# Moving GpSimd's share of the states, the bf16 parts' transfers and the end-state copies of a selective scan

## The chip, the cores and the metric

The kernel runs on one core of one Trainium2 chip. The metric is the device time of one execution in microseconds (us). The core has five engines with a queue each: TensorE (PE), VectorE (DVE), ScalarE (ACT), GpSimd (POOL) and SyncE (SP, which only issues transfers). Each works its own queue in order and waits for the others by semaphores.

## The reference, cut to what matters

The whole network is an attention block, a sigmoid recurrence, a state-space block (Mamba) run forward and backward over 16384 tokens, and a two-of-eight expert block, each added to the input. The change touches only the state-space block, whose core is, for 128 inner channels and 16 states each:

```python
dt = softplus(dt @ dt_w.T + dt_b)
A = -exp(A_log)
dA = exp(dt[..., None] * A)
dBx = dt[..., None] * Bm[:, :, None, :] * xc[..., None]
def step(h, inp):
    dA_t, dBx_t, C_t = inp
    h = dA_t * h + dBx_t
    y = einsum('bds,bs->bd', h, C_t)
...
y = ys + xc * D
y = y * silu(z)
return y @ out_w.T
...
y_fwd + flip(mamba(flip(x)))
```

## The kernel before, in words

`scan_direction` is called twice, for the forward direction (tile names begin with `sf_`) and then the backward one (`sb_`). The 16384 tokens are cut into 16 chunks of 1024 (`TC`). Channels lie on the 128 partitions, tokens along the free axis. A chunk has 16 **units**, one for each state s. A unit consists of

- the decays exp(dt·A[s]), by ACT: `decay_v` (L1361) into the ring `dA`, three units ahead, or `decay_g` (L1366) into the PSUM buffer `pu`, one unit ahead;
- the inputs dt·x·B[s]. For the ten states in `BY_V`, PE spreads row s of B over the partitions with two bf16 matmuls into `pu` (`spread_b`, L1212), and DVE multiplies by `dtx` in place (`inject`, L1501). For the six states in `BY_G`, a transfer brings B's row spread into `bb`, and POOL multiplies into `dbx` (`inject`, L1436), two units ahead;
- the recurrence itself, by DVE: a scan instruction (L1521) that starts from `state[:, s]` and writes `h`, a ring of four;
- the product with C's row, by POOL: `read_c` (L1443) of unit s-1, into `hc`, a ring of four;
- the sum over the states, by PE: `total` (L1232), two matmuls with the identity into `py`, four units behind;
- the last column of `h`, kept for the next chunk, by ACT: `keep` (L1373).

`pu` has two PSUM buffers, used by s modulo 2. So `spread_b` and `decay_g` of unit s wait until the scan of unit s-2 is done; `spread_b` of unit 1 therefore waits for scan 15 of the chunk before.

Between the units stands the work that prepares the next chunk (`prepare`), with its place given by a unit number. The order on an engine is: the unit's own instructions, then `prepare`, then `tail`, then `own`. PE: the convolution (L1182, unit 0), B and C (`in_out`, units 2 and 3), the step size (units 5 and 6). ACT: `silu_x` after unit 1, in the backward direction `silu_z` too, between two table loads (L1285, L1292), since Silu and Exp are in different tables; `bc_rows` (4), `load_flat` (5), `part_high` (6), three pieces of softplus (7 and 8), `part_middle` (9), `store_parts` and `take_dt` (11), `load_parts` (12). POOL: `part_rest` (7), `linear_and_log` (9, L1417), `part_low` (10). DVE: `lost` (9), `step_sum` (10, L1476, which waits for POOL's `linear_and_log`), `dt_x` (12, L1482). B's rows are split into three bf16 parts, stored to memory and loaded back in another layout (`store_parts`, `load_parts`) for the matmuls of `spread_b`.

In the backward direction DVE also does `gate` (L1488) behind unit 3: it multiplies the finished y of the chunk before by silu(z). Only then may PE begin the next y. It does so in unit 4: the join with the forward y (L1224), the product with D (L1229) and `total` of unit 0; behind it stands the gate's matmul (`gate_in`, L1167). `project` (L1246) follows unit 13 on PE, `add_x` (L1494) unit 14 on DVE. In the forward direction ACT copies y out behind unit 3 (`take_y`).

The numbers that set the order:

```python
C_RING, B_RING, DECAY_RING = 4, 3, 5
DECAY_AHEAD, INJECT_AHEAD, LAG_SUM = 3, 2, 4
BY_G = (2, 5, 7, 10, 13, 15)
```

Of the kernel before, what the change touches and what calls it, by code (L numbers as in the profile page):

```python
# [24 lines left out]
def need(eng, sem, count):  # L25

    if not (isinstance(count, int) and count <= 0):
        eng.wait_ge(sem, count)  # L28
# [902 lines left out]
RING = 4  # L931
C_RING, B_RING, DECAY_RING = 4, 3, 5
DECAY_AHEAD, INJECT_AHEAD, LAG_SUM = 3, 2, 4
BY_G = (2, 5, 7, 10, 13, 15)
# [131 lines left out]
def scan_direction(nc, c, nd, k, way, y_scratch, rows, split):  # L1066
# [5 lines left out]
    U = STATES  # L1072
    NV, NG_ = len(BY_V), len(BY_G)
    with ExitStack() as ctx:
# [11 lines left out]
        h, hc = sb("h", [128, RING, TC]), sb("hc", [128, RING, TC])  # L1086
# [32 lines left out]
        def after(n, par, s):  # L1119

            return (n, par, s) if s < U else (n + 1, 1 - par, s - U)
# [153 lines left out]
        def _(act):  # L1275
# [88 lines left out]
            def decay_g(n, par, s):  # L1364
                need(act, scanned, n * U + s - 1)
                nc.scalar.activation(p_u[s % 2][:, :], dt[:, par, :], ACT.Exp,  # L1366
                                     scale=k["A"][:, s:s + 1]).then_inc(g_decayed, 1)

            def keep(n, s):

                act.wait_ge(scanned, n * U + s + 1)
                e = 0 if back else TC - 1
                nc.scalar.copy(state[:, s:s + 1], h[:, s % RING, e:e + 1]).then_inc(kept, 1)  # L1373
# [8 lines left out]
            def unit(n, par, s, first, last):  # L1382
                if first and s == 0:
                    for j in range(DECAY_AHEAD):
                        if j in BY_V:
                            decay_v(0, 0, j)
                m, mpar, ms = after(n, par, s + 1)
                if ms in BY_G and not (last and s == U - 1):
                    decay_g(m, mpar, ms)
                m, mpar, ms = after(n, par, s + DECAY_AHEAD)  # L1390
                if ms in BY_V and not (last and s + DECAY_AHEAD >= U):
                    decay_v(m, mpar, ms)
                if s >= 2:
                    keep(n, s - 2)
                elif not first:
                    keep(n - 1, s - 2 + U)
# [3 lines left out]
                       (8, softplus_exp), (8, softplus_one), (8, softplus_log), (9, part_middle), (11, store_parts),  # L1400
                       (11, take_dt), (12, load_parts)]
# [63 lines left out]
        def _(dve):  # L1465
# [38 lines left out]
            def unit(n, par, s, first, last):  # L1504
                if first and s == 0 and s in BY_V:
                    inject(0, 0, 0)
                u = n * U + s
                flow = lambda t: t[:, ::-1] if back else t[:, :]
                need(dve, kept, u + 1 - RING)
# [353 lines left out]
```

## Time and profile before

| what | us |
|---|---|
| median of 3 runs (2959.31 to 2975.59) | 2970.94 |
| the profiled execution | 2967.89 |
| its span in the profile | 2966.1 |
| PE busy | 2497.7 (84%) |
| DVE busy | 2318.3 (78%) |
| POOL busy | 2084.2 (70%) |
| ACT busy | 1576.8 (53%) |

The forward scans run from 851 to 1714 us of the span and the backward ones from 1763 to 2682 us, together about 60% of the time; everything outside them is unchanged. The busy shares over the whole span mix stages, so the two directions are to be read each for itself.

### The profile page before, as it was taken

To read this page: it belongs to the slowest core of one execution; us is meant where nothing else is said; L and a number is where in the kernel's file an instruction comes from. 1 tells how busy PE (TensorE), PEld (TensorE's weight loads), DVE (VectorE), ACT (ScalarE), POOL (GpSimd) and SP (SyncE) were. 2 spreads that over 40 slices of the span, in tenths; PEclk is the share of its full clock that TensorE was granted. 3 is DMA by queue.
4 is the path that set the end of the run, shared out by engine and by line. 5 is a ranking of instruction groups with operands and counts; after the bars stand their busy time and mean duration, and the time that the engine had idled before them with its cause. 6 is when DMAs were issued, how large, how long until landed. Compare 5 with 4: busy or idle time off the path is not lost. (4 is left out here: it accounts for less than half of the span.)

```text
span 2966.1 us, 34800 instructions
## 1 busy us (share of the span) xinstructions
PE 2497.7 (84%) x7800; PEld 1190.2 (40%) x7800; DVE 2318.3 (78%) x2487; ACT 1576.8 (53%) x2784; POOL 2084.2 (70%) x1166
## 2 busy tenths in 40 slices
PE   7899999957468988889889858899889889988598
PEld 7666666624322323323323223333333333336422
DVE  4366666560659999999999939998999899895499
ACT  6466666543655655555656446555555555545221
POOL 3133333230359999999999949999999999995155
PEclk6699999969779999999999889999999999997599
DMA  3000000000256777777777637776766676660022
GB/s 60 8 9 9 9 9 9 6 1 0 59 167 223 243 244 237 247 235 240 246 236 241 227 124 235 219 236 216 229 226 222 221 225 224 218 211 17 13 54 47
DMA packets 177295, 437.72 MB, mean 148 GB/s; under 512 B 65638, under 2 KB 70219, under 8 KB 177228
## 3 DMA queue, kind: packets, MB, share of 16 engines
q1 hardware_dynamic: 139340, 420.19, 44.5%
q10 hardware_dynamic: 37888, 16.79, 2.1%
q8 instruction: 24, 0.39, 0.1%
q14 instruction: 43, 0.35, 0.0%
HBM read 404.40 MB, written 24.12 MB: 144 GB/s over the span
## 5 line engine op out<-in xcount | busy, mean ns | idle before, releaser
L1443 POOL TENSOR_TENSOR sb_hc<-sb_h,sb_cc 128x1024 f32<-128x1024 f32 x256 | 599.7, 2360 | 61.8 <-PE sb_py L1232 56.2
L1443 POOL TENSOR_TENSOR sf_hc<-sf_h,sf_cc 128x1024 f32<-128x1024 f32 x256 | 595.8, 2347 | 11.5 <-DVE sf_h L1521 8.2
L1232 PE MATMUL sf_py<-sf_hc,ident 128*128 128x512 f32 x1024 | 533.1, 655 | 0.6 <-POOL sf_hc L1443 0.6
L1232 PE MATMUL sb_py<-sb_hc,ident 128*128 128x512 f32 x1024 | 519.5, 638 | 0.0
L572 POOL TENSOR_TENSOR ar_sc<-ar_sc,ar_mx 128x512 f32<-128x512 f32 x128 | 154.7, 1208 | 356.6 <-DVE ar_mx L513 356.6
L1521 DVE TENSOR_TENSOR_SCAN sf_h<-sf_dA,sf_state,sf_pu 128x1024 f32<-128x1024 f32 x160 | 375.4, 2346 | 19.1
L1521 DVE TENSOR_TENSOR_SCAN sb_h<-sb_dA,sb_state,sb_pu 128x1024 f32<-128x1024 f32 x160 | 375.2, 2345 | 17.1
L1232 PEld LDWEIGHTS sf_py<-sf_hc,ident 128*128 128x128 f32 x1024 | 197.0, 205 | 269.3 <-issue 239.8
L1232 PEld LDWEIGHTS sb_py<-sb_hc,ident 128*128 128x128 f32 x1024 | 187.3, 196 | 241.0 <-issue 232.0
L1501 DVE TENSOR_TENSOR sb_pu<-sb_pu,sb_dtx 128x1024 f32<-128x1024 f32 x160 | 193.9, 1212 | 52.7 <-PE sb_pu L1212 52.7
L1436 POOL TENSOR_TENSOR sb_dbx<-sb_dtx,sb_bb 128x1024 f32<-128x1024 f32 x96 | 226.5, 2359 | 3.3 <-DVE sb_dtx L1482 3.3
L1436 POOL TENSOR_TENSOR sf_dbx<-sf_dtx,sf_bb 128x1024 f32<-128x1024 f32 x96 | 225.2, 2346 | 3.3 <-DVE sf_dtx L1482 3.3
L1521 DVE TENSOR_TENSOR_SCAN sf_h<-sf_pu,sf_state,sf_dbx 128x1024 f32<-128x1024 f32 x96 | 223.7, 2330 | 1.8 <-ACT sf_state L1373 1.7
L1521 DVE TENSOR_TENSOR_SCAN sb_h<-sb_pu,sb_state,sb_dbx 128x1024 f32<-128x1024 f32 x96 | 223.9, 2332 | 0.0
L1212 PE MATMUL sf_pu<-sf_bcs,ss_sel 48*128 48x512 bf16 x320 | 104.9, 411 | 133.8 <-DVE sf_h L1521 117.0
L1361 ACT ACTIVATE sf_dA<-sf_dt,ss_A 128x1024 f32<-128x1024 f32 x160 | 182.3, 1141 | 55.6 <-DMA split_scratch<-sf_parts 47.4
L1361 ACT ACTIVATE sb_dA<-sb_dt,ss_A 128x1024 f32<-128x1024 f32 x160 | 182.4, 1141 | 53.7 <-DMA split_scratch<-sb_parts 40.3
L1501 DVE TENSOR_TENSOR sf_pu<-sf_pu,sf_dtx 128x1024 f32<-128x1024 f32 x160 | 194.0, 1212 | 10.4 <-PE sf_pu L1212 9.6
L1212 PE MATMUL sb_pu<-sb_bcs,ss_sel 48*128 48x512 bf16 x320 | 100.4, 396 | 116.1 <-DVE sb_h L1521 97.0
L1366 ACT ACTIVATE sf_pu<-sf_dt,ss_A 128x1024 f32<-128x1024 f32 x96 | 107.3, 1117 | 154.3 <-DVE sf_h L1521 119.0
L1366 ACT ACTIVATE sb_pu<-sb_dt,ss_A 128x1024 f32<-128x1024 f32 x96 | 107.2, 1117 | 148.8 <-DVE sb_h L1521 148.6
L508 DVE TENSOR_TENSOR ar_sc<-ar_pss,at_bias 128x512 f32<-128x512 f32 x128 | 88.5, 692 | 121.7 <-PE ar_pss L443 120.0
(294 smaller groups left out, 4594.6 us busy)
## 6 DMA issues: line engine op xcount, KB each, us to landing
sf_cc<-rows_scratch SPq DMA_DIRECT2D x256, 512.0 KB, 4.4
sb_cc<-rows_scratch SPq DMA_DIRECT2D x256, 512.0 KB, 4.4
sf_bb<-rows_scratch SPq DMA_DIRECT2D x96, 512.0 KB, 5.4
sb_bb<-rows_scratch SPq DMA_DIRECT2D x96, 512.0 KB, 5.4
sf_n<-n_scratch SPq DMA_DIRECT2D x32, 258.0 KB, 5.4
sb_n<-n_scratch SPq DMA_DIRECT2D x32, 258.0 KB, 5.3
y_scratch<-sf_yo SPq DMA_DIRECT2D x16, 512.0 KB, 6.1
sb_yf<-y_scratch SPq DMA_DIRECT2D x16, 512.0 KB, 5.1
```

The costliest lines, as they stand in the source:

```text
L508: nc.vector.tensor_tensor(sc[:, j, :, :], ps_s[:, j % 2, :, :], bias[:, :, :], ALU.add).then_inc(added, 1)
L572: nc.gpsimd.tensor_tensor(sc[:, j, :, :], sc[:, j, :, :], mx[:, j, :].rearrange("p (h a) -> p h a", a=1).to_broadcast([128, HEADS, 128]), ...
L1212: ins = nc.tensor.matmul(p_u[s % 2][:, hf], lhsT=k["sel"][:, s:s + 1].to_broadcast([3 * STATES, 128]), rhs=bcs[:, par, hf], start=True, st ...
L1232: ins = nc.tensor.matmul(p_y[:, hf], lhsT=c.ident[:, :], rhs=hc[:, s % RING, hf], start=False, stop=(s == U - 1))
L1361: nc.scalar.activation(dA[:, BY_V.index(s) % DECAY_RING, :], dt[:, par, :], ACT.Exp, scale=k["A"][:, s:s + 1]).then_inc(v_decayed, 1)
L1366: nc.scalar.activation(p_u[s % 2][:, :], dt[:, par, :], ACT.Exp, scale=k["A"][:, s:s + 1]).then_inc(g_decayed, 1)
L1436: nc.gpsimd.tensor_tensor(dbx[:, r % B_RING, :], dtx[:, par, :], bb[:, r % B_RING, :], ALU.mult).then_inc(g_injected, 1)
L1443: nc.gpsimd.tensor_tensor(hc[:, s % RING, :], h[:, s % RING, :], cc[:, s % C_RING, :], ALU.mult).then_inc(read, 1)
L1501: nc.vector.tensor_tensor(p_u[s % 2][:, :], p_u[s % 2][:, :], dtx[:, par, :], ALU.mult).then_inc(v_injected, 1)
L1521: nc.vector.tensor_tensor_scan(out=flow(h[:, s % RING, :]), data0=flow(decays), data1=flow(inputs), initial=state[:, s:s + 1], op0=ALU.mul ...
```

## The change

GpSimd's six states become 0, 3, 6, 9, 11 and 14. ACT keeps end states two at a time, in every odd unit, ahead of `decay_v` instead of behind it. `take_dt` goes ahead of `store_parts`, which goes from unit 11 to unit 12, and `load_parts` from 12 to 14.

```diff
-BY_G = (2, 5, 7, 10, 13, 15)
+BY_G = (0, 3, 6, 9, 11, 14)
...
             def decay_g(n, par, s):
+                if s == 0:
+                    act.wait_ge(dt_done, n + 1)
                 need(act, scanned, n * U + s - 1)
...
-                act.wait_ge(scanned, n * U + s + 1)
+                act.wait_ge(scanned, n * U + s + 2)
                 e = 0 if back else TC - 1
-                nc.scalar.copy(state[:, s:s + 1], h[:, s % RING, e:e + 1]).then_inc(kept, 1)
+                nc.scalar.copy(state[:, s:s + 2], h[:, s % RING:s % RING + 2, e]).then_inc(kept, 1)
...
                 if ms in BY_G and not (last and s == U - 1):
                     decay_g(m, mpar, ms)
+                if s % 2 and s >= 3:
+                    keep(n, s - 3)
+                elif s % 2 and not first:
+                    keep(n - 1, s - 3 + U)
                 m, mpar, ms = after(n, par, s + DECAY_AHEAD)
                 if ms in BY_V and not (last and s + DECAY_AHEAD >= U):
                     decay_v(m, mpar, ms)
-                if s >= 2:
-                    keep(n, s - 2)
-                elif not first:
-                    keep(n - 1, s - 2 + U)
...
-                       (8, softplus_exp), (8, softplus_one), (8, softplus_log), (9, part_middle), (11, store_parts),
-                       (11, take_dt), (12, load_parts)]
+                       (8, softplus_exp), (8, softplus_one), (8, softplus_log), (9, part_middle),
+                       (11, take_dt), (12, store_parts), (14, load_parts)]
...
-                need(dve, kept, u + 1 - RING)
+                if s % 2 == 0:
+                    need(dve, kept, n * PAIRS + (s - RING) // 2 + 1)
```

Lines of the changed kernel are one to six higher than those of before.

ScalarE, backward direction, around the two table loads of a chunk. Before:

```order
L1366 ACTIVATE sb_pu<-sb_dt,ss_A 128x1024
L1361 ACTIVATE sb_dA<-sb_dt,ss_A 128x1024
L1373 COPY sb_state<-sb_h 128x1
L1285 ACT_TABLE_LOAD
L1285 ACTIVATE sb_xc<-sb_pp,ss_cb 128x1024
L1289 ACTIVATE sb_zs<-sb_zs 128x1024
L1292 ACT_TABLE_LOAD
L1373 COPY sb_state<-sb_h 128x1
L1361 ACTIVATE sb_dA<-sb_dt,ss_A 128x1024
```

The same place in the changed kernel:

```order
L1362 ACTIVATE sb_dA<-sb_dt,ss_A 128x1024
L1376 COPY sb_state<-sb_h 128x2
L1362 ACTIVATE sb_dA<-sb_dt,ss_A 128x1024
L1286 ACT_TABLE_LOAD
L1286 ACTIVATE sb_xc<-sb_pp,ss_cb 128x1024
L1290 ACTIVATE sb_zs<-sb_zs 128x1024
L1293 ACT_TABLE_LOAD
L1369 ACTIVATE sb_pu<-sb_dt,ss_A 128x1024
L1362 ACTIVATE sb_dA<-sb_dt,ss_A 128x1024
```

The decays into `pu` next to this place were those of unit 2, ahead of the table loads; now they are those of unit 3, right behind them.

TensorE, backward direction, where the next y begins (L1224, L1225). Before:

```order
L1201 MATMUL sb_pp<-sb_xc,ss_wbc 32x512
L1224 MATMUL sb_py<-sb_yf,ident 128x512 x2
L1229 MATMUL sb_py<-sb_xc,ss_dg 128x512 x2
L1232 MATMUL sb_py<-sb_hc,ident 128x512 x2
L1167 MATMUL sb_pp<-sb_n,ss_wz 128x512 x2
L1212 MATMUL sb_pu<-sb_bcs,ss_sel 128x512 x2
L1232 MATMUL sb_py<-sb_hc,ident 128x512 x2
```

The same place in the changed kernel:

```order
L1202 MATMUL sb_pp<-sb_xc,ss_wbc 32x512
L1213 MATMUL sb_pu<-sb_bcs,ss_sel 128x512 x2
L1225 MATMUL sb_py<-sb_yf,ident 128x512 x2
L1230 MATMUL sb_py<-sb_xc,ss_dg 128x512 x2
L1233 MATMUL sb_py<-sb_hc,ident 128x512 x2
L1168 MATMUL sb_pp<-sb_n,ss_wz 128x512 x2
L1233 MATMUL sb_py<-sb_hc,ident 128x512 x2
```

The spread of B's row for the next DVE state (`pu`) stood behind the new y (unit 6); now one stands ahead of it (unit 5) and the next one follows further down (unit 7).

GpSimd, backward direction, the second half of a chunk. Before:

```order
L1436 TENSOR_TENSOR sb_dbx<-sb_dtx,sb_bb 128x1024
L1443 TENSOR_TENSOR sb_hc<-sb_h,sb_cc 128x1024 x3
L1423 TENSOR_TENSOR sb_rest<-sb_flat,sb_parts 128x128
L1436 TENSOR_TENSOR sb_dbx<-sb_dtx,sb_bb 128x1024
L1443 TENSOR_TENSOR sb_hc<-sb_h,sb_cc 128x1024 x2
L1417 TENSOR_TENSOR sb_tc<-sb_tc,sb_tb 128x1024
```

The same place in the changed kernel:

```order
L1448 TENSOR_TENSOR sb_hc<-sb_h,sb_cc 128x1024 x3
L1441 TENSOR_TENSOR sb_dbx<-sb_dtx,sb_bb 128x1024
L1448 TENSOR_TENSOR sb_hc<-sb_h,sb_cc 128x1024
L1428 TENSOR_TENSOR sb_rest<-sb_flat,sb_parts 128x128
L1448 TENSOR_TENSOR sb_hc<-sb_h,sb_cc 128x1024
L1441 TENSOR_TENSOR sb_dbx<-sb_dtx,sb_bb 128x1024
L1448 TENSOR_TENSOR sb_hc<-sb_h,sb_cc 128x1024
L1422 TENSOR_TENSOR sb_tc<-sb_tc,sb_tb 128x1024
```

Before, `dbx` of unit 7 stood ahead of the three reads of units 4, 5 and 6, and `dbx` of unit 10 between the reads and `linear_and_log` (`sb_tc`). Now the reads of units 3, 4 and 5 come first, and both `dbx` of unit 9 and `dbx` of unit 11 stand between the read of unit 5 and `linear_and_log`.

## Rows read from the trace of the kernel before

**Rows 1.** Windows, forward and backward scans: busy us of each engine, PEclk, DMA

```profile
900.00:1700.00 800.00, 690.89 (x1524) 243.99 (x1524) 761.76 (x428) 450.74 (x670) 795.19 (x368) 0.93 0.73 239
1800.00:2640.00 840.00, 741.42 (x1833) 285.96 (x1832) 774.12 (x450) 465.14 (x666) 788.34 (x364) 0.95 0.69 224
```

**Rows 2.** Waits, 1860 to 2580: who waited, us in total, times, longest

```profile
ACT sb_dt L1322 <- POOL sb_parts L1428: 57.0, 12, 4.8
POOL sb_hc L1443 <- PE sb_py L1232: 44.4, 44, 1.9
DVE sb_pu L1501 <- PE sb_pu L1212: 40.7, 12, 3.4
```

**Rows 3.** Timeline of DVE, one backward chunk: start us, us, instruction, idle before

```profile
2234.04 1.22 DVE L1488 TENSOR_TENSOR sb_yo<-sb_py,sb_zs 128x1024 f32<-128x1024 f32 x1 [0.57 <-PE sb_py L1232]
2235.18 2.34 DVE L1521 TENSOR_TENSOR_SCAN sb_h<-sb_dA,sb_state,sb_pu 128x1024 f32<-128x1024 f32 x1
2237.44 2.32 DVE L1521 TENSOR_TENSOR_SCAN sb_h<-sb_pu,sb_state,sb_dbx 128x1024 f32<-128x1024 f32 x1
2243.19 1.23 DVE L1501 TENSOR_TENSOR sb_pu<-sb_pu,sb_dtx 128x1024 f32<-128x1024 f32 x1 [3.43 <-PE sb_pu L1212]
...
2260.80 1.22 DVE L1476 TENSOR_TENSOR sb_pp<-sb_tc,sb_pp 128x1024 f32<-128x1024 f32 x1
...
2265.52 2.35 DVE L1521 TENSOR_TENSOR_SCAN sb_h<-sb_dA,sb_state,sb_pu 128x1024 f32<-128x1024 f32 x1
...
2275.34 2.34 DVE L1521 TENSOR_TENSOR_SCAN sb_h<-sb_pu,sb_state,sb_dbx 128x1024 f32<-128x1024 f32 x1
...
2291.77 1.21 DVE L1488 TENSOR_TENSOR sb_yo<-sb_py,sb_zs 128x1024 f32<-128x1024 f32 x1
```

**Rows 4.** Timeline of PE, the same backward chunk

```profile
2222.71 3.60 PE L1182 MATMUL sb_pp<-sb_n,ss_taps 128*128 128x512 f32 x8
...
2235.40 1.98 PE L1224 MATMUL sb_py<-sb_yf,ident 128*128 128x512 f32 x4 [0.52 <-DVE sb_yo L1488]
...
2240.74 1.98 PE L1167 MATMUL sb_pp<-sb_n,ss_wz 64*128 64x512 f32 x4
2242.56 0.59 PE L1212 MATMUL sb_pu<-sb_bcs,ss_sel 48*128 48x512 bf16 x2
2243.09 1.98 PE L1232 MATMUL sb_py<-sb_hc,ident 128*128 128x512 f32 x4
```

**Rows 5.** Timeline of ACT, the same backward chunk

```profile
2226.47 1.28 ACT L1285 ACT_TABLE_LOAD   x1 [1.26 <-PE sb_pp L1182]
2227.76 1.11 ACT L1285 ACTIVATE sb_xc<-sb_pp,ss_cb 128x1024 f32<-128x1024 f32 x1
...
2229.84 1.28 ACT L1292 ACT_TABLE_LOAD   x1
...
2232.39 1.12 ACT L1366 ACTIVATE sb_pu<-sb_dt,ss_A 128x1024 f32<-128x1024 f32 x1
```

**Rows 6.** Timeline of POOL, the same backward chunk

```profile
2245.22 2.36 POOL L1443 TENSOR_TENSOR sb_hc<-sb_h,sb_cc 128x1024 f32<-128x1024 f32 x1 [1.92 <-PE sb_py L1232]
...
2250.49 2.38 POOL L1436 TENSOR_TENSOR sb_dbx<-sb_dtx,sb_bb 128x1024 f32<-128x1024 f32 x1
...
2257.45 2.37 POOL L1417 TENSOR_TENSOR sb_tc<-sb_tc,sb_tb 128x1024 f32<-128x1024 f32 x1
```

**Rows 7.** Timeline of POOL, one forward chunk

```profile
1211.27 2.34 POOL L1417 TENSOR_TENSOR sf_tc<-sf_tc,sf_tb 128x1024 f32<-128x1024 f32 x1
...
1250.94 6.97 POOL L1443 TENSOR_TENSOR sf_hc<-sf_h,sf_cc 128x1024 f32<-128x1024 f32 x3
```

**Rows 8.** Timeline of DVE, the same forward chunk

```profile
1213.65 1.23 DVE L1476 TENSOR_TENSOR sf_pp<-sf_tc,sf_pp 128x1024 f32<-128x1024 f32 x1 [0.44 <-POOL sf_tc L1417]
```

**Rows 9.** Timeline of PE, the same forward chunk

```profile
1230.21 0.60 PE L1212 MATMUL sf_pu<-sf_bcs,ss_sel 48*128 48x512 bf16 x2
...
1246.48 1.88 PE L1232 MATMUL sf_py<-sf_hc,ident 128*128 128x512 f32 x4
```

More of the change, by code:

```diff
@@ L1073, in scan_direction @@
     NV, NG_ = len(BY_V), len(BY_G)
+    PAIRS = U // 2
     with ExitStack() as ctx:
@@ L1383, in unit @@
                 if first and s == 0:
+                    if s in BY_G:
+                        decay_g(0, 0, s)
                     for j in range(DECAY_AHEAD):
```

## The prediction, made before the changed kernel was run

> **What bounds the kernel now.** I read the page first: no engine is busy over the whole span, and the chain that ended last runs through the experts' stage and says nothing here. So I took windows of the two scan directions [rows 1]. Forward, POOL is busy for 795 of 800 us: it sets the pace, and nothing that frees another engine can make this direction faster, since POOL's work is the same before and after (22 products and the three pieces for the next chunk). Backward, POOL (788 of 840) and DVE (774) both have gaps. The waits say why [rows 2]: POOL waits for PE's y sums, 44.4 us in 12.5 chunks, and DVE once in each chunk, for 3.4 us, for PE's spread of B. The timelines show this place. DVE does `gate` at 2234.04 [rows 3]; only then PE begins the next y, at 2235.40, then comes `gate_in` at 2240.74, and then the spread of unit 6, at 2242.56 [rows 4]. Meanwhile DVE has only scans 4 and 5 and stands until 2243.19. From one gate to the next are 2291.77 - 2234.04 = 57.73 us, my backward period. It is made of 26.76 (gate to `step_sum` at 2260.80), 4.72 (to scan 12), 9.82 (to scan 15) and 16.43 (to the gate).
>
> **Prices.** A scan holds DVE for 2.26 (2235.18 to 2237.44). From scan 15 to the gate are five scans and four injects, so these take 16.43 - 5 x 2.26 = 5.13: 1.34 for an inject whose own scan follows at once, 1.12 with something else between. A POOL product takes 2.32 (2250.49 to 2257.45 are three) [rows 6]; its short pieces, about 0.4, are in both orders. On PE a spread takes 0.53 and a sum of four records 1.82 [rows 4]. A `decay_g` takes 1.12 on ACT [rows 5].
>
> **The change, part by part.**
>
> *Behind the gate, DVE.* It now has scan 4, inject 5, scan 5 and scan 6 ahead of the first inject (7) that needs a spread behind the new y: 2.26 + 1.34 + 2.26 + 2.26 = 8.1 us in place of 4.5. But that spread also stands further back, behind the sum of unit 1 and a step-size half (about 0.9). So PE frees inject 7 not 9.1 us after the gate's start but about 11.9, and the wait is 11.9 - 1.1 - 8.1 = 2.7 instead of 3.4. This is all that the regular spacing wins there, 0.7 us, and only if DVE is what sets the period.
>
> *Behind the gate, POOL.* The read of unit 5 needs the sum of unit 1. That sum now follows `gate_in` directly: gate + 1.36 + 5.34 + 1.82, and the read starts 2.13 behind the sum's start [rows 4, 6], at gate + 10.65 (before: 11.18). Then POOL has read 5, product 9, read 6, the rest piece, read 7, product 11, read 8: six products and 0.4, or 14.3 us, one product more than before, because the product of 7 used to be done while POOL waited. `linear_and_log` starts at gate + 24.95, and `step_sum` 2.38 behind its start (as forward, 1211.27 to 1213.65 [rows 7, 8]): gate + 27.33 instead of 26.76. **+0.6.** DVE alone, freed at gate + 11.9, would be there 1.4 us earlier, so its 0.7 is lost again.
>
> *From `step_sum` to scan 12*: one scan, one inject and the sum itself in both, 4.72. *From scan 12 to scan 15*: DVE gets injects 13 and 15 where it had 14: 2.26 + 1.12 + 1.12 + 2.26 + 2.26 + 1.12 + 0.6 (`add_x`) = 10.74 instead of 9.82. **+0.9.** It is paid back with one inject fewer behind scan 15, if nothing stops DVE there.
>
> *From scan 15 to the gate.* Something does. PE may spread unit 1 only when scan 15 is done, 2.41 us after its start; spread and a sum (0.53 + 1.82) put the convolution at +4.76. ACT's first table load came 3.76 behind the convolution's start (2222.71 to 2226.47), the second 3.37 later, and what follows it 1.29 later [rows 4, 5]. Before, no decay that DVE needs soon stood behind: that of unit 2 was ahead of the loads. Now `decay_g` of unit 3 is the first instruction behind them: 4.76 + 3.76 + 3.37 + 1.29 + 1.12 = 14.3 us after scan 15's start, when scan 3 may begin. DVE's own work would be there after four scans and two injects, 4 x 2.26 + 2.68 = 11.7. So DVE waits 2.6 for ACT, in a place where it never waited. (PE's spread of unit 2, now behind the convolution, is late by 0.7 too; the longer wait holds it.) Then scan 3 and inject 4: the gate is at 14.3 + 2.26 + 1.12 = 17.7 instead of 16.43. **+1.3.**
>
> Sum backward: 27.33 + 4.72 + 10.74 + 17.7 = 60.5, against 57.73: **+2.8 a chunk**.
>
> *The table loads, by a page.* Rows 5 show the load itself at 1.28 and the next ACTIVATE 1.29 behind its start. The Trainium skill, "ScalarE: Activation LUTs", section "What ACT_TABLE_LOAD costs", gives about 2.66 us for every switch, drain included. With two switches ahead of `decay_g` of unit 3 the wait would be 2.8 longer (an estimate from that page), a period of 63.3. The row speaks against it; it is rival D.
>
> *Forward.* Counted from the start of `linear_and_log` (1211.27), read 4 of the next chunk started at 1250.94, +39.67 [rows 7], with POOL never idle. In the new order one product fewer stands before it, so POOL is there at +37.36. It needs the sum of unit 0. Before, from the spread of unit 1 (1230.21) to that sum's end (1246.48 + 1.88) PE needed 18.15 without a gap [rows 9]; now there is one spread more in it (unit 5), 18.7. The spread starts at 2.38 (`step_sum` [rows 8]) + 15.1 (`step_sum` itself, scans 11 to 14, injects 12, 13 and 15 and `dt_x`: 1.12 + 4 x 2.26 + 1.34 + 1.12 + 1.12 + 1.34) + 2.41 = +19.9, before +18.94. The sum ends at 38.6 and POOL reads at 38.7: POOL waits 1.4 us where it had 2.6 us in hand. Nothing gives it back. DVE's wait for `decay_g` of unit 3 is 1.5 here (no silu of z between the tables), and its cycle of about 53.9 stays under 55.3. **+1.4 a chunk** on 53.9.
>
> *The rest.* `take_dt` no longer waits for POOL's last part; it waited 57.0 us in 12.5 chunks [rows 2], but dt is ready by scan 12 in both orders, so this is worth nothing on the path. The two transfers of the parts are still issued from ACT's queue, a unit or two later, and what stands behind `load_parts` there is `decay_g` of unit 0, needed three scans later; PE first needs the parts for unit 1 of the next chunk, after scan 15. I take nothing for it; if the store had not landed by unit 14, its remainder would go straight onto scan 0. Half as many `keep`s free a little of ACT, which it doesn't need. The two-at-a-time wait asks, ahead of scan s, for the copy of scan s-3, and ACT gets to it within one unit: nothing again. Without that cover a late copy could hold each even scan by up to a decay's 1.12.
>
> **The sum.** Sixteen chunks have 15 intervals in a direction; the first starts with empty rings, so I count 14. Backward 14 x 2.8 = 39, forward 14 x 1.4 = 20: 2968 + 59 = 3027 for the profiled execution, which is 3 under the median. With a microsecond or so off each direction's start (scan 0 no longer needs the bf16 parts) I say **3025**.
>
> **The rivals.**
> A, the forecast, 0.50: 3005 to 3045 as the terms come out 40% smaller or larger.
> B, only the backward direction slows, 0.16: forward POOL's 1.4 us is a difference of sums of 38 us, and PE's clock and gaps can move it by that much. 2968 + 39 = 3007.
> C, scan 3 doesn't wait for ACT (convolution or silu is earlier than I place it), 0.12: then only PE's 0.7 at unit 2 is left there, the gate is at 15.9, the period 58.7, +1.0 a chunk or 14, with 0 to 20 forward: 2982 to 3002, say 2992.
> E, even, 0.10: POOL's waits behind the gate end as they did; 2968.
> F, faster, 0.10: one mechanism, DVE's longer cover behind the gate. If neither `step_sum` nor scan 3 waits, DVE sets the period and wins 0.7 a chunk, 14 x 0.7 = 10, 2958; if PE frees inject 7 before DVE is there, 3.4 x 14 = 48, 2920. It decides from the point where PE needs less than 9.2 us from the gate's start to the spread of unit 7; the rows give 11.9.
> D, the page's table switch, 0.02: backward 5.6 and forward about 2.8 a chunk, 3085.
>
> **How the numbers follow.** A, B and C and part of E lie within **2970 to 3045**, which leaves out F, D and the edges. A measurement of this kernel can tell about 0.5% (15 us) from no change. Faster by more: most of F, 0.08. Within: E, the rest of F and the low end of C, 0.14. Slower by more: 0.78.
>
> **What would show it.** Right: in the backward chunk a wait of DVE at scan 3 for ACT's decay, some 2 to 3 us, that isn't there before; a wait of about 1 us at `step_sum` for POOL; the wait for the spread still 2 to 3 us, now at inject 7; POOL's waits for the sums at reads 4 and 5 up from 3.4 to over 6 us; a period of about 60.5. Forward, POOL busy 97 to 98% instead of 99.4%, with one wait of 1 to 1.5 us for PE, period about 55.3. Wrong: scans back to back through units 0 to 3, or POOL still full forward. The weakest step is the place of the convolution against scan 15: all of +1.3 hangs on it, and the forward term on the same spread of unit 1.

## The result and the profile after

The changed kernel takes 3052.66 us (median of four runs, 3040.46 to 3054.44) against 2965.12 of the kernel before on the same chip (2951.19 to 2975.59): ratio 1.029, 95% interval 1.024 to 1.034. It is slower, as forecast, but by 3% instead of 2%; the time is 8 us above the top of the range. The profiled execution has a span of 3052.7 us, 86.6 more than before. In a second set the ratio was 1.029 again (1.025 to 1.034).

The windows of the two directions, with the columns of [rows 1]. POOL is busy for 769 of 800 us forward, where it was busy for 795, and for 653 of 740 us backward, where it was busy for 788 of 840:

```profile
900.00:1700.00 800.00, 684.24 (x1477) 243.19 (x1478) 736.55 (x414) 429.22 (x540) 769.28 (x357) 0.92 0.70 230
1900.00:2640.00 740.00, 642.80 (x1543) 242.96 (x1544) 643.89 (x376) 375.82 (x459) 653.26 (x303) 0.93 0.65 212
```

The waits, 1900 to 2640, answer to [rows 2]: who waited, us in total, times, longest.

```profile
POOL sb_hc L1448 <- PE sb_py L1233: 86.7, 36, 4.5
...
ACT sb_dt L1323 <- DVE sb_pp L1481: 50.4, 12, 4.2
...
DVE sb_pu L1506 <- PE sb_pu L1213: 49.6, 24, 2.7
...
DVE sb_h L1527 <- ACT sb_pu L1369: 21.1, 12, 1.8
...
DVE sb_pp L1481 <- POOL sb_tc L1422: 15.7, 12, 1.3
```

The last two are new: once in each chunk at scan 3 for ACT's decay (1.8), and once at `step_sum` for POOL (1.3). `take_dt` now waits for DVE, no longer for POOL's parts. One backward chunk and the first scans of the next, on DVE; it answers to [rows 3]:

```profile
2217.57 2.34 DVE L1527 TENSOR_TENSOR_SCAN sb_h<-sb_dA,sb_state,sb_pu 128x1024 f32<-128x1024 f32 x1
...
2226.57 1.23 DVE L1506 TENSOR_TENSOR sb_pu<-sb_pu,sb_dtx 128x1024 f32<-128x1024 f32 x1 [0.81 <-PE sb_pu L1213]
...
2232.04 2.35 DVE L1527 TENSOR_TENSOR_SCAN sb_h<-sb_pu,sb_state,sb_dbx 128x1024 f32<-128x1024 f32 x1 [1.75 <-ACT sb_pu L1369]
...
2235.43 1.21 DVE L1493 TENSOR_TENSOR sb_yo<-sb_py,sb_zs 128x1024 f32<-128x1024 f32 x1
...
2247.37 1.23 DVE L1506 TENSOR_TENSOR sb_pu<-sb_pu,sb_dtx 128x1024 f32<-128x1024 f32 x1 [2.63 <-PE sb_pu L1213]
...
2262.73 1.23 DVE L1481 TENSOR_TENSOR sb_pp<-sb_tc,sb_pp 128x1024 f32<-128x1024 f32 x1 [1.30 <-POOL sb_tc L1422]
...
2267.47 2.35 DVE L1527 TENSOR_TENSOR_SCAN sb_h<-sb_dA,sb_state,sb_pu 128x1024 f32<-128x1024 f32 x1
...
2278.18 2.35 DVE L1527 TENSOR_TENSOR_SCAN sb_h<-sb_dA,sb_state,sb_pu 128x1024 f32<-128x1024 f32 x1
...
2288.76 1.23 DVE L1506 TENSOR_TENSOR sb_pu<-sb_pu,sb_dtx 128x1024 f32<-128x1024 f32 x1 [2.39 <-PE sb_pu L1213]
...
2294.23 2.35 DVE L1527 TENSOR_TENSOR_SCAN sb_h<-sb_pu,sb_state,sb_dbx 128x1024 f32<-128x1024 f32 x1 [1.76 <-ACT sb_pu L1369]
...
2297.61 1.22 DVE L1493 TENSOR_TENSOR sb_yo<-sb_py,sb_zs 128x1024 f32<-128x1024 f32 x1
```

From scan 15 at 2217.57 to the gate at 2235.43 are 17.86 us, from the next scan 15 (2278.18) to its gate (2297.61) 19.43. The two passages of scan 15 on PE show where the 1.57 us are:

```profile
2220.06 0.59 PE L1213 MATMUL sb_pu<-sb_bcs,ss_sel 48*128 48x512 bf16 x2 [0.94 <-DVE sb_h L1527]
2220.58 1.98 PE L1233 MATMUL sb_py<-sb_hc,ident 128*128 128x512 f32 x4
2222.40 3.60 PE L1183 MATMUL sb_pp<-sb_n,ss_taps 128*128 128x512 f32 x8
...
2280.58 0.89 PE L1213 MATMUL sb_pu<-sb_bcs,ss_sel 48*128 48x512 bf16 x2 [1.98 <-DVE sb_h L1527]
2281.40 3.35 PE L1233 MATMUL sb_py<-sb_hc,ident 128*128 128x512 f32 x4
2284.59 3.60 PE L1183 MATMUL sb_pp<-sb_n,ss_taps 128*128 128x512 f32 x8
```

The same spread and the same sum take 2.3 us once and 4.0 the next time; the convolution starts 4.83 and 6.41 behind scan 15. The granted clock of the two stretches (the last number but two):

```profile
2218.00:2222.00 4.00, 3.06 (x9) 1.02 (x8) 4.00 (x2) 1.52 (x3) 4.00 (x3) 1.00 0.56 134
2280.50:2284.60 4.10, 4.02 (x7) 1.53 (x8) 3.97 (x4) 1.24 (x2) 4.10 (x3) 0.58 0.95 351
```

The first is all at 2.4 GHz, the second mostly at 1.2, which I call half clock from here on; a chunk or period without it on the path I call clean. ACT, and with it scan 3, is late by the same amount. In front of scan 3 ACT shows what was forecast, compare [rows 5]:

```profile
2226.16 1.28 ACT L1286 ACT_TABLE_LOAD   x1 [4.96 <-PE sb_pp L1183]
...
2229.53 1.28 ACT L1293 ACT_TABLE_LOAD   x1
2230.82 1.12 ACT L1369 ACTIVATE sb_pu<-sb_dt,ss_A 128x1024 f32<-128x1024 f32 x1
```

I took every interval from one `step_sum` to the next in the two traces. Backward, before, they are 57.6 to 57.7 or, in every second chunk from the sixth on, 58.4 to 58.5, but for the first (57.3); after, they are 60.6 or 62.27, from the third on in turn, but for the first (58.9) and the last (60.9). In all seven of 60.6 the convolution starts 4.8 us behind scan 15, in all five of 62.27 it starts 6.4 behind. In the first and the last ACT's first table load runs ahead of the convolution's end, 3.6 us behind scan 15, and scan 3 waits for ACT only 0.38 us instead of 1.76. Forward, after, five of 14 are 55.3, with the convolution at 4.8; nine are 56.1 or 57.0, with it at 5.4 to 6.5. The whole span, in us:

| stretch | before | after | more | forecast |
|---|---|---|---|---|
| start to the first `step_sum` | 844.5 | 851.3 | 6.7 | 0 |
| first forward interval | 41.9 | 44.0 | 2.2 | 0 |
| 14 forward intervals | 758.7 | 786.5 | 27.8 | 20 |
| to the first backward `step_sum` | 111.2 | 107.1 | -4.1 | 0 |
| first backward interval | 41.9 | 48.0 | 6.1 | 0 |
| 14 backward intervals | 810.7 | 855.5 | 44.7 | 39 |
| the rest | 357.2 | 360.3 | 3.2 | 0 |

### The profile page after: what moved, and what is told of

The parts are those of the page before. It is cut to its first block and busy times, and to the rows that moved or that the text cites. A ratio compares the mean times of both kernels' runs of the same rounds, so it can differ in the third digit from the quotient of the medians.

```text
span 3052.7 us, 34204 instructions
## 1 busy us (share of the span) xinstructions
PE 2549.1 (84%) x7800; PEld 1211.6 (40%) x7800; DVE 2317.0 (76%) x2487; ACT 1549.3 (51%) x2530; POOL 2082.5 (68%) x1166
## 5 line engine op out<-in xcount | busy, mean ns | idle before, releaser
L1448 POOL TENSOR_TENSOR sb_hc<-sb_h,sb_cc 128x1024 f32<-128x1024 f32 x256 | 600.0, 2356 | 111.2 <-PE sb_py L1233 107.7
L1233 PE MATMUL sb_py<-sb_hc,ident 128*128 128x512 f32 x1024 | 533.9, 661 | 0.0
L1233 PEld LDWEIGHTS sb_py<-sb_hc,ident 128*128 128x128 f32 x1024 | 197.8, 206 | 270.6 <-issue 262.0
L1369 ACT ACTIVATE sf_pu<-sf_dt,ss_A 128x1024 f32<-128x1024 f32 x96 | 107.1, 1116 | 158.6 <-DVE sf_h L1527 156.4
```

The costliest lines, as they stand in the source:

```text
L1233: ins = nc.tensor.matmul(p_y[:, hf], lhsT=c.ident[:, :], rhs=hc[:, s % RING, hf], start=False, stop=(s == U - 1))
L1448: nc.gpsimd.tensor_tensor(hc[:, s % RING, :], h[:, s % RING, :], cc[:, s % C_RING, :], ALU.mult).then_inc(read, 1)
```

## The experiments

Ratios are to the kernel before in the same set (medians there 2960.6 to 2964.1). "F" and "B" are the sums of the 14 forward and 14 backward intervals of a kernel's trace: 758.7 and 810.7 before, 786.5 and 855.5 after. Ahead of these intervals most experiments change nothing, and yet the first `step_sum` lay between 837 and 855 us: differences under some 10 us of the whole are read from F and B, not from the time.

**The places alone.** The kernel before with the six new places and nothing else but what they need.

```diff
-BY_G = (2, 5, 7, 10, 13, 15)
+BY_G = (0, 3, 6, 9, 11, 14)
@@ decay_g
+                if s == 0:
+                    act.wait_ge(dt_done, n + 1)
```

> The kernel before with only GpSimd's units moved to 0, 3, 6, 9, 11, 14 (and the wait of unit 0's decay that this needs). My theory: the places alone make the whole loss, by what they put behind the table loads, behind the gate and ahead of linear_and_log: about 3050 us, forward period 55.3 to 57, backward 60.6 to 62.3. Rival: the moved store, load and take_dt or the end states kept in pairs carry a part of it: below 3030.

Measured: ratio 1.023 (1.021 to 1.025), F 786.4, B 849.4. By this trace the places carry all of F's loss and 39 of B's 45; by the medians, 72 of the 88 us. The profiled execution is the longest of the four (3054.0; the others 3030.0 to 3039.7), so the split is rough. Its backward chunks are also of two kinds that the changed kernel doesn't mix like this. In six, ACT's first table load stands behind the convolution, scan 3 waits 1.76, and the clean period is 60.6, as in the changed kernel. In eight, the load runs while ACT waits for the convolution, scan 3 waits 0.35, and the clean period is 59.2:

```profile
2348.85 1.28 ACT L1285 ACT_TABLE_LOAD   x1
2354.74 1.11 ACT L1285 ACTIVATE sb_xc<-sb_pp,ss_cb 128x1024 f32<-128x1024 f32 x1 [4.60 <-PE sb_pp L1182]
...
2413.99 1.28 ACT L1285 ACT_TABLE_LOAD   x1 [5.94 <-PE sb_pp L1182]
2415.28 1.11 ACT L1285 ACTIVATE sb_xc<-sb_pp,ss_cb 128x1024 f32<-128x1024 f32 x1
```

Half clock in five chunks (60.9 to 64.0) makes up for it. An estimate from the clean periods alone, 8 x 59.2 + 6 x 60.6 = 837, gives the places 30 and ACT's queue 11 of the 42 us by which clean backward chunks grew. Why the load stands now ahead of ACT's wait and now behind it isn't shown.

**ACT's queue alone.** The changed kernel with the old places.

```diff
-BY_G = (0, 3, 6, 9, 11, 14)
+BY_G = (2, 5, 7, 10, 13, 15)
```

> The changed kernel with GpSimd's units back at 2, 5, 7, 10, 13, 15, so only ScalarE's queue is changed (store_parts, load_parts, take_dt, end states in pairs, kept ahead of decay_v). My theory: nothing, within 8 us of the kernel before, periods 53.9 and 57.6 to 58.5. Rival: a part of the loss is here, 10 us or more above it; or a gain, now that ACT does not stand 4.8 us ahead of dt.

Measured: ratio 1.001 (0.9995 to 1.003), F 753.8, B 810.6, periods 53.9 and 57.6 / 58.4. The later transfers, the kept pairs and the earlier `take_dt` are worth nothing here as a whole; F is 5 us shorter than before, all of it in one interval (53.0 for 57.85, the one with half clock described further down). With the new places the queue adds 6 us to B (849.4 to 855.5): scan 3 waits 1.76 for ACT in 12 of 14 chunks, instead of 0.96 on average (1.76 in six, 0.35 in eight).

**The table loads one unit later**, behind the decay of unit 3.

```diff
-            prepare = [(1, silu_x), ...
+            prepare = [(2, silu_x), ...
-                run(act, unit, prepare, [(1, silu_z)], [(1, exp_log_tables), (5, take_z)])
+                run(act, unit, prepare, [(2, silu_z)], [(2, exp_log_tables), (5, take_z)])
```

> The changed kernel with silu_x, silu_z and the second table load placed after unit 2 instead of unit 1, so that the decay of unit 3 stands ahead of them. My theory: DVE's wait for that decay (1.76 us backward, 0.7 to 0.8 forward) is gone, the backward gate comes 1.3 us sooner until PE's late spreads and sums stop it, forward nothing since POOL's read of unit 4 binds: 3030 to 3040 us. Rival: the wait is cover for PE's late spread and its removal only lengthens the wait at the gate or at inject 7: 3050.

Measured: ratio 1.024 (1.022 to 1.026), F 786.4, B 840.9. DVE waits for ACT no more; clean backward periods fall from 60.6 to 59.4, by 1.2 of the 1.3 that the forecast had put there. There are five of these. Eight others are 60.6 again: there the convolution is at 5.4 to 6.5, and DVE waits 2.5 us at inject 2 instead of 0.74.

**`linear_and_log` one unit earlier.**

```diff
-            run(pool, unit, [(7, part_rest), (9, linear_and_log), (10, part_low)])
+            run(pool, unit, [(7, part_rest), (8, linear_and_log), (10, part_low)])
```

> The changed kernel with POOL's linear_and_log after unit 8 instead of unit 9, so ahead of dbx of unit 11 and the read of unit 8. My theory: step_sum no longer waits for POOL (1.3 us backward, 1.0 forward); backward DVE wins 1.3 a chunk; forward DVE gets ahead by 1 us, so spread 1, sum 0 and POOL's read 4 come sooner and the period falls from 55.3 to about 54.2: together 3015 us. Rival: POOL's time to log is not there earlier or the time is lost again at the gate: 3045 to 3052.

Measured: ratio 1.020 (1.017 to 1.024), F 786.0, B 836.4, clean backward periods 59.2. The wait at `step_sum` is gone, and clean periods are 1.4 shorter: the 0.6 of the forecast against the kernel before, and the 0.7 and more that DVE alone could have won ("1.4 us earlier"). Forward the third to the eighth period are 54.2 to 54.8, but from the ninth on they are 57.3 to 58.2: POOL now waits for ACT's softplus, 28.0 us in 10 chunks.

**The changed kernel again**, as the reference of the next three.

> The changed kernel again, unaltered, as the reference for the three others of this call. Both theories: about 3040 to 3055 us, ratio to before 1.024 to 1.030, periods 55.3 to 57.0 forward and 60.6 / 62.3 in turn backward. How far its clean periods and its whole time differ from the first run shows how much of the whole time is not in the chunks.

Measured: 3050.02 us, ratio 1.029 (1.025 to 1.034), F 786.6, B 855.4, the same alternation.

**Zero matmuls against the clock, first try.** They add zeros to the running y.

```diff
+            def fill(s):
+                if s in (1, 12, 13, 15):
+                    for _ in range(6):
+                        nc.tensor.matmul(p_y[:, 0:HALF], lhsT=nil[:, 0:128], rhs=nil[:, :], start=False, stop=False)
@@ spread_b
+                fill(s)
                 need(pe, scanned, n * U + s - 1)
```

> The changed kernel with six matmuls of a zero tile, added into the running y (they add zeros), ahead of the spreads of units 1, 12, 13 and 15 in every chunk, where PE stands idle. Clock theory (the 1.6 us that every second chunk takes beyond the forecast is PE at half its clock behind these gaps, on the path from scan 15 over the spread of unit 1 and the convolution to ACT and scan 3): periods uniform, 55.3 forward and 60.6 backward, no stretch of these chunks with PEclk near 0.5, the 14 intervals 786 -> 775 forward and 855 -> 848 backward, time 18 us or so lower, 3030 to 3038. Rival (the alternation is a beat of waits between the engines, and the clock only follows): periods alternate as before whatever the clock says, time unchanged or some us longer, as the zero matmuls delay the spread by what they overhang.

Measured: ratio 1.036 (1.032 to 1.041), F 801.0, B 863.3. A miss. Six take 1.47 us. Ahead of unit 1 that is a little more than PE's idle time: backward the convolution is at 5.1 in most chunks, and behind scan 15 the clock is full there, as wanted. But in four chunks DVE waits 4.3 to 4.4 us at inject 7 instead of 2.7, since now the join of y behind the gate runs partly at half clock (3.51 us at 2120.86 instead of 1.98). Forward, from the seventh period on, the convolution is at 7.4 to 7.5 and the periods are 57.9 to 58.1.

The same in the kernel before, ahead of units 0, 1, 12 and 14:

> The kernel before with the same zero matmuls, ahead of the spreads of units 0, 1, 12 and 14. Clock theory: the backward periods, 57.64 and 58.45 in turn, become 57.64 throughout, so 5 to 6 us less, and forward stays at 53.9, where POOL is never idle: ratio 0.998. Rival: no change in the alternation. With this and the run above the cost of the change at a full clock can be read: 2.9 a chunk backward and 1.4 forward by the forecast's terms, 60 us, against 72 measured in the chunks.

Measured: ratio 1.023 (1.019 to 1.028), F 766.5, B 854.4. Also a miss: ahead of units 0 and 1 PE wasn't idle at all here, and backward the convolution is at 6.4 to 8.3 behind scan 15 instead of 5.0. It shows something else, though. With 2.6 us more on PE ahead of the convolution (two fills of 1.3) B is 44 longer, 3 a chunk (60.2 in two chunks, 61.4 to 61.5 in eleven in which half clock came on top): PE's stretch behind scan 15 was nearly on the path before, too.

**Table loads and `linear_and_log` together.** The edits of the third and fourth experiment.

> The changed kernel with both waits that the forecast named put off: the table loads and silus one unit later (behind the decay of unit 3) and POOL's linear_and_log one unit earlier (unit 8). Alone, the first gave 841 backward and 786 forward over 14 intervals, the second 836 and 786. If the two terms are independent and add (the forecast's sum: +1.3 at scan 3, +0.6 at step_sum): backward 855 - 15 - 19 = 821, forward 786, time about 3013 to 3020. Rival (each was only the last of several waits, and PE's y sums and spreads behind the gate come next): backward stays near 836 and the time near 3024.

Measured: ratio 1.023 (1.019 to 1.027), F 809.3, B 815.2, most backward periods 57.9 to 58.1. Backward both waits are gone, and 40 of the 45 us come back, more than the 15 and 19 of each alone. Forward POOL waits for ACT, 50.4 us in 13 chunks.

**The convolution first.** In PE's queue it goes ahead of the spread of unit 1, into the time in which PE waits for scan 15.

```diff
             def unit(n, par, s, first, last):
+                if s == 0 and not last:
+                    for step in (convolve(halves[0]), convolve(halves[1])):
+                        step(n + 1, 1 - par)
                 m, mpar, ms = after(n, par, s + 1)
@@ in the loop over units (ahead of it the steps stay)
-            prepare = [(0, convolve(a)), (0, convolve(b)), (2, in_out(a)), (3, in_out(b)),
+            prepare = [(-1, convolve(a)), (-1, convolve(b)), (2, in_out(a)), (3, in_out(b)),
```

> The changed kernel with one move on PE: the next chunk's convolution stands ahead of the spread of unit 1, which waits for scan 15, instead of behind that spread and the sum after it. So it fills PE's gap of 0.9 to 2.0 us there, and neither the sum of 1.98 us (3.35 at half clock) nor the wait for scan 15 lies between it and ACT's table loads any more; what it overhangs makes the spread of unit 1 about 1.5 to 2 us later. Theory (backward: scan 3 waits for ACT behind the convolution, and the 1.6 us of every second chunk is the half clock of the sum on this path; forward: POOL waits for the sum of unit 0 at the end of PE's chain from scan 15): no wait of DVE for ACT at scan 3, backward periods 58.8 to 59.4 without the alternation, 14 intervals 823 to 832 instead of 855; forward POOL full again, periods 53.9 to 54.5, 14 intervals 755 to 763 instead of 786; time about 3000. Rival 1 (the alternation is a beat between POOL and PE behind the gate): the backward periods still alternate by about 1.6. Rival 2 (forward, the six-product order itself costs POOL 1.4): forward stays near 786 and the time near 3025.

Measured: ratio 1.010 (1.007 to 1.013), F 775.3, B 813.9: backward more than expected, forward less. Backward the period is 57.8 to 58.1 in all chunks but the first, without the alternation by 1.6, and DVE has no wait for ACT. Half clock is still there. In the last seven chunks it takes in all of PE's work from the spread of unit 12 to the `...` here (granted clock 0.57 from 2226.0 to 2237.5), though no longer the two sums just ahead of the convolution:

```profile
2226.07 1.03 PE L1213 MATMUL sb_pu<-sb_bcs,ss_sel 48*128 48x512 bf16 x2 [2.51 <-DVE sb_h L1530]
2227.03 3.78 PE L1233 MATMUL sb_py<-sb_hc,ident 128*128 128x512 f32 x4
2230.86 1.03 PE L1213 MATMUL sb_pu<-sb_bcs,ss_sel 48*128 48x512 bf16 x2
2231.83 5.70 PE L1233 MATMUL sb_py<-sb_hc,ident 128*128 128x512 f32 x8
...
2239.72 3.70 PE L1233 MATMUL sb_py<-sb_hc,ident 128*128 128x512 f32 x8
2243.26 3.60 PE L1183 MATMUL sb_pp<-sb_n,ss_taps 128*128 128x512 f32 x8
2246.79 0.60 PE L1213 MATMUL sb_pu<-sb_bcs,ss_sel 48*128 48x512 bf16 x2
```

These chunks are 58.0 to 58.1, the six before them, with less of it, 57.8 to 57.9. So half clock costs next to nothing by itself: it costs where PE is on the path. Forward five periods are 54.0 to 54.3, as POOL alone would have it, the others up to 57.3: the theory's gain came in a third of the chunks.

**The same in the kernel before.**

> The kernel before with the same move of the convolution. Forward POOL is never idle, so nothing: 53.9. Backward, by the clock theory, the alternation of 57.64 and 58.45 ends at 57.64 or a little less: 14 intervals 807 or under instead of 810.7, ratio 0.998 to 1.000. Rival (the later spread of unit 1 is needed at once by inject 1 or holds POOL's next sum): backward 1 to 2 us a chunk longer, ratio 1.005 to 1.01.

Measured: ratio 1.013 (1.009 to 1.016), F 760.3, B 833.1. The rival: backward inject 1 waits 0.8 to 2.2 us for the later spread; most periods are 58.6, and three times 61.7 with 60.0 behind it, where half clock comes on top. The old places want the spread of unit 1 at once.

**Convolution first, `linear_and_log` earlier in the backward direction alone.**

```diff
-            run(pool, unit, [(7, part_rest), (9, linear_and_log), (10, part_low)])
+            run(pool, unit, [(7, part_rest), (8 if back else 9, linear_and_log), (10, part_low)])
```

> The first kernel of this call with POOL's linear_and_log one unit earlier (8 for 9) in the backward direction alone. With silu and linear_and_log moved together the backward periods were 57.9 to 58.1 throughout, 815 in 14 intervals, though the forward ones rose to 58 from a new wait. Theory: both waits that the forecast named are gone here without that side effect: backward 812 to 818, forward 755 to 763, time 2985 to 2992, still not under before, since PE frees the inject behind the gate as late as before (57.6 or so a chunk). Rival (with DVE's five units behind the gate the period falls under that of before once the two waits are gone, the case F of the forecast): backward under 807, time under 2980.

Measured: ratio 1.009 (1.006 to 1.012), F 773.1, B 812.6, periods of 56.48 and 59.58 in strict turn. The chunk of 59.58 on PE, just ahead of its convolution:

```profile
2293.53 0.60 PE L1213 MATMUL sb_pu<-sb_bcs,ss_sel 48*128 48x512 bf16 x2 [2.51 <-DVE sb_h L1530]
2294.06 3.34 PE L1233 MATMUL sb_py<-sb_hc,ident 128*128 128x512 f32 x4
...
2305.00 1.03 PE L1213 MATMUL sb_pu<-sb_bcs,ss_sel 48*128 48x512 bf16 x2
2305.96 6.49 PE L1233 MATMUL sb_py<-sb_hc,ident 128*128 128x512 f32 x8
2312.28 3.60 PE L1183 MATMUL sb_pp<-sb_n,ss_taps 128*128 128x512 f32 x8
```

In the chunk of 56.48 the two sums ahead of the convolution take 3.70, here 6.49; DVE then stands 3.06 us at inject 1 for the spread behind it, where it doesn't wait in the short chunk.

**The mixed kernel.** Forward the old places and the old order, backward as in the last kernel.

```diff
+    BY_G = (0, 3, 6, 9, 11, 14) if back else (2, 5, 7, 10, 13, 15)
+    BY_V = tuple(s for s in range(16) if s not in BY_G)
```

> Forward as in the kernel before (its places of GpSimd's units, the convolution behind the first sum), backward as in the last kernel of the call before (new places, convolution first, linear_and_log at unit 8), where chunks of 56.5 and 59.6 took turns. Theory: forward 753 to 759 in 14 intervals, backward 812 or so, first backward interval 48 instead of 42; time 2968 to 2980, the same as before within what can be told. Rival (the forward half clocks and the queue changes cost here too): over 2985.

Measured: 2968.38 us, ratio 1.002 (1.000 to 1.003), F 753.8, B 803.5. Six periods are 56.4 to 56.5 in a row, then come six of 58.0 to 58.1 and one of 56.7. The backward instructions stand in the same order as in the kernel just above, with B = 812.6: 9 us apart by where half clock fell. Against the kernel before, B is 7 us shorter, the first backward interval 5.6 longer (47.5), and the whole the same, as expected.

**Zero matmuls only in idle time**, first in the mixed kernel (backward):

```diff
+                for _ in range({12: 11, 13: 3}.get(s, 0) if back else 0):
```

> The same with zero matmuls in the backward direction where TensorE stands idle: eleven ahead of the spread of unit 12 (idle 2.51) and three ahead of that of unit 13 (0.85). Clock theory: chunks of 56.5 throughout, 14 intervals 791 to 796 instead of 812, time 2948 to 2960, which is the case F of the forecast with its two waits and the clock taken away. Rival (59.6 isn't from the clock, or filled gaps don't hold the clock up): 812 or more, time as the mixed kernel without fills or above it.

Measured: ratio 1.003 (1.002 to 1.005), B 812.5, periods 56.5 and 59.6 in strict turn: no gain. The fill ended half clock behind units 12 and 13, but in every second chunk the two sums just ahead of the convolution still take 6.5 us instead of 3.7.

Then in the kernel before, ahead of units 11, 12 and 14 (`{11: 5, 12: 3, 14: 15}`):

> The kernel before with zero matmuls only where TensorE is idle: five ahead of the spread of unit 11 (idle 1.33), three ahead of unit 12 (0.85), fifteen ahead of unit 14 (3.87). Clock theory: backward periods 57.64 throughout (14 intervals 807 instead of 810.7), forward 53.9, granted clock of these windows up from 0.94 and 0.95, time 4 us lower. Rival: the half clock comes all the same, periods 57.64 and 58.45 in turn.

Measured: ratio 1.002 (1.000 to 1.004), F 757.0, B 811.2. Eleven of the 13 last backward periods are 57.6 to 57.7, but one is 58.95 and one 60.68. Half clock still came once with only 0.53 us idle, right behind fifteen zero matmuls:

```profile
2257.25 3.41 PE L1209 MATMUL sb_py<-sb_nil 48*128 48x512 bf16 x15
2261.18 1.03 PE L1219 MATMUL sb_pu<-sb_bcs,ss_sel 48*128 48x512 bf16 x2 [0.53 <-DVE sb_h L1530]
```

And in the changed kernel, `{12: 11, 13: 5, 1: 4}`:

> The changed kernel with zero matmuls only where TensorE is idle: eleven ahead of the spread of unit 12 (2.51), five ahead of unit 13 (1.3 to 2.3), four ahead of unit 1 (0.9 to 2.0). Clock theory: periods 55.3 and 60.6 throughout, 14 intervals 775 and 848 instead of 787 and 855, time 3030 to 3036. Rival: the alternation stays and the time is 3050 or above.

Measured: ratio 1.032 (1.026 to 1.037), F 788.1, B 858.8. The convolution now starts 4.75 behind scan 15 in 13 of 14 backward chunks, and most periods still are 60.6 and 62.2 in turn; forward the fill delays it to 5.6 to 7.2 in eight chunks. PE at another place of the long chunk, the join of y behind the gate, and DVE behind it:

```profile
2246.30 3.68 PE L1232 MATMUL sb_py<-sb_yf,ident 128*128 128x512 f32 x4 [1.59 <-DVE sb_yo L1502]
...
2258.67 1.23 DVE L1515 TENSOR_TENSOR sb_pu<-sb_pu,sb_dtx 128x1024 f32<-128x1024 f32 x1 [4.32 <-PE sb_pu L1220]
```

The join takes 3.68 in place of 1.98, and the wait at inject 7 is 4.32 in place of 2.70. The half clock has moved from one place of the path to another.

## Why the prediction was right in direction and too low

**Which case.** A, waits in both directions, is what happened; its range of 3005 to 3045 ended too low.

**Gate to `step_sum`** was 27.33, measured 27.30 (2235.43 to 2262.73). Its cause, six products of POOL behind the late sum, stands in the wait of 1.30 and in the fourth experiment. (POOL's waits for the sums at reads 4 and 5 are 4.42 and 1.48 us, 5.9 together; over 6 was expected.) DVE alone would be there 1.4 us earlier, as forecast. **`step_sum` to scan 12**: 4.72, measured 4.74. **Scan 12 to scan 15**: 10.74, measured 10.71. **Scan 15 to the gate**: 17.7, measured 17.86 in a clean chunk. The wait of 2.6 came as 0.81 at inject 2 and 1.75 at scan 3; the forecast gave all of it to scan 3. Scan 3 starts at 14.47 (forecast 14.3). The sum, 60.5, is 60.62 in clean chunks. **Behind the gate** the wait for the spread is 2.63 at inject 7 (forecast 2.7). **Forward** 55.3, measured 55.27 in clean chunks; the forecast's own difference, 38.7 - 37.36, is 1.34 and not 1.4, and 1.34 is what clean chunks show.

Clean against clean, 14 x (60.62 - 57.65) + 14 x (55.27 - 53.93) = 60.3 us, where the forecast had 59. Rivals B, C and E fall with it. F's mechanism does exist, though not in this change: with both waits gone and the convolution first, clean chunks last 56.4 to 56.5, under the 57.65 before; in no kernel were all chunks like that.

**The step that failed** is the convolution's place against scan 15, "spread and a sum (0.53 + 1.82) put the convolution at +4.76", taken as the same in every chunk. The forecast named this step its weakest, but gave TensorE's clock no term; rival B mentions it, as something that could take away 1.4 us, not add. In every second backward chunk the spread and sum run at half clock, on the path, and the convolution is at +6.4. Before, half clock also came, backward in every second chunk from the sixth on, but there it cost 0.8 us:

```profile
2209.40:2214.00 4.60, 4.55 (x7) 1.66 (x8) 4.49 (x3) 2.43 (x4) 4.60 (x3) 0.50 0.69 242
```

Forward, before, it cost something in one chunk alone: in the interval of 57.85 PE ran at a granted clock of 0.50 from 900.5 to 909.7, and DVE waited 3.91 us for a spread. In the others POOL set the pace. The new places put this stretch of PE on the path in both directions, with the whole delay. What lies above the clean periods is 6.8 backward (before 3.6) and 12.7 forward (before 3.7, all of it in that one interval): 12 us net.

The Trainium skill, "TensorE: Matmul & The Clock Gate", Part 1 on the clock gate, says that the number of slow matmuls varies from run to run with the phase of the gate. The traces agree: in two executions of the changed kernel the longer forward intervals fall on different chunks (the fourth is the first of them in one, the third in the other), and two kernels with one backward order, the mixed one and the one before it, had B of 803.5 and 812.6.

**The remainder.** Of 86.6 us the forecast had 59. Missing are 12 for the clock, 1.3 in the clean periods, 8 in the first intervals and 6 outside the chunks. The 6 can't be told from chance: the forward scans' first instruction, ahead of which nothing was changed, already runs at 814.7 before and 822.3 after, and between 808 and 825 in the 17 traces.

The 8 are a second step that failed: "with a microsecond or so off each direction's start" measured 2.2 and 6.1 more. The first backward interval is 46.6 to 49.0 in every kernel with the new places backward, and 41.9 to 42.8 with the old ones in the old order. Most of it is one wait, 4.5 to 5.3 us in all kernels with the new places, where the kernel before has none at inject 6 or 7 of this interval:

```profile
1821.46 1.23 DVE L1506 TENSOR_TENSOR sb_pu<-sb_pu,sb_dtx 128x1024 f32<-128x1024 f32 x1 [4.53 <-PE sb_pu L1213]
```

There is no gate in this interval. PE begins the join of y 19.6 us behind the `step_sum` instead of 16.5, since now the spread of unit 5, which waits for scan 3, stands ahead of it, and the join takes 3.78 us instead of 1.98. The other waits are 0.75 at inject 2 for PE and 1.35 at the next `step_sum` for POOL. The kernel before with the convolution first (46.9) has waits for PE at other places, 3.23 at inject 1 and 1.59 at inject 6.

**The range.** By its own rule, terms 40% larger, it would have ended at 2968 + 1.4 x 59 = 3051. Its top of 3045 allows for 30%. The measured time is 2 us above the former and 8 above the latter.

**Right on the rest with the old places alone**: there the later transfers, the kept pairs and `take_dt` cost nothing. With the new ones, for which the forecast took nothing for them either, they cost 6 us of B by the traces and 11 by the estimate from clean periods, all at scan 3. The clean period came out right because the chain had the first table load behind the convolution, as it stood in the kernel before; with the places alone it stands there in only six of 14 chunks. To that extent the 60.5 was luck.

**The table loads.** Both take 1.28 us, and `decay_g` starts 1.29 behind the second. So rival D, by which a switch costs the 2.66 us of the Trainium skill, "ScalarE: Activation LUTs", section "What ACT_TABLE_LOAD costs", is not seen here: its period of 63.3 appears in no chunk.

**What stays open**: what makes the clock fall in one chunk and not in the next. That the long chunks are those with half clock on the path is shown by the intervals, by the convolution first, where the alternation ended, and by the first and the last fill of the changed kernel, where the half clock moved and the wait with it. That filling PE's idle time gives time back is refuted as far as tried: in the changed kernel the mean granted clock rose (0.886 to 0.903 over the span), and the time didn't fall.

## What to carry to other kernels

A regular spacing of an engine's share is no gain by itself: what counts is which work stands between a release (the gate, scan 15) and the first instruction that waits for what it releases, on every queue. The terms of such a chain could be read to 0.2 us from the trace of before; so ask also whether the chain now passes through TensorE behind one of its idle gaps, and price that stretch at both clock levels. Where two waits follow each other, take both away before judging an order: each alone gave 15 to 19 us of B, both together 40.

## What the runs showed of the hardware

- The same spread and sum on TensorE took 2.3 us at a granted clock of 1.00 and 4.0 at 0.58, in adjacent chunks, behind 0.94 and 1.98 us of idle time. Idle time doesn't tell it alone: behind 2.51 us the spread took 0.60 in one kernel (2293.53) and 1.03 in another (2226.07), and 1.03 behind 0.53 us of idle time and fifteen zero matmuls.
- The pattern can repeat from period to period: 60.6 and 62.27 in turn, at the same chunks in two executions; 56.48 and 59.58 in two kernels.
- Of two kernels with one backward order, one had six short periods in a row, the other never two: 9 us.
- ScalarE's table load of 1.28 us can run while ScalarE waits for the input of the ACTIVATE behind it (2348.85, with 4.60 us of waiting after it), or only after that wait (2413.99), within one kernel; scan 3 then waits 0.35 or 1.76 us.
